# Local attention: queries in rows, the sum as a 65th column, and results transposed for the output

## What is computed

```python
def local_attention(q, k, v):           # per head; window of 128 queries, 256 keys
    sim = einsum('bhwid,bhwjd->bhwij', bq, bk)
    mask = (i < j) | (i > j + WINDOW) | (j == -1)
    sim = where(mask, -finfo.max, sim)
    attn = softmax(sim, axis=-1)
    out = einsum('bhwij,bhwjd->bhwid', attn, bv)
...
h = shift_token(x); q, k, v = split(h @ wqkv, 3)
q, k = l2norm(q) * qs, l2norm(k) * ksc; q, k = rotary_xpos(q, k)
x = x + local_attention(q, k, v) @ wo
x = x + feed_forward(x)                 # layer norm, w1, gelu gate, w2
```

## Time and profile before

| | |
|---|---|
| median of 3 runs (lowest to highest) | 1937.51 us (1932.22 to 1951.54) |
| the profiled execution, its time | 1935.36 us |
| its span from the first instruction to the last | 1933.9 us |
| TensorE clock granted, mean | 0.937 of 2.4 GHz |
| PE busy | 1773.7 us (92%) |
| PE weight loads busy | 1350.9 us (70%) |
| DVE, ACT, POOL busy | 1146.3 (59%), 982.9 (51%), 862.8 us (45%) |

### The profile page before, as it was taken

How to read it: one execution, slowest core, us unless ns; L and a number is a source line. 1 busy time by engine, 2 the same in 40 slices (tenths; PEclk the granted TensorE clock), 3 DMA queues, 4 the chain that set the end, 5 groups by cost and what they waited for, 6 DMA issues and landing times. The chain is left out here.

```text
span 1933.9 us, 42804 instructions
## 1 busy us (share of the span) xinstructions
PE 1773.7 (92%) x14072; PEld 1350.9 (70%) x14072; DVE 1146.3 (59%) x2863; ACT 982.9 (51%) x1898; POOL 862.8 (45%) x895
## 2 busy tenths in 40 slices
PE   6999999999569999999969999689999999879997
PEld 4566665666347777777758888467777777678886
DVE  5567766667367667666633333666666776325554
ACT  2655656655336555555543444345555655434443
POOL 3333334333246655555632333445556665325544
PEclk7888989998679999999988999889999999979999
DMA  5333344334010000000021222201000000212221
GB/s 149 108 109 121 105 131 123 115 111 132 22 35 12 33 33 33 33 33 22 0 89 55 65 65 88 66 12 33 33 33 1 32 33 22 78 54 77 87 87 44
DMA packets 103736, 121.29 MB, mean 63 GB/s; under 512 B 23386, under 2 KB 75780, under 8 KB 103684
## 3 DMA queue, kind: packets, MB, share of 16 engines
q1 hardware_dynamic: 96772, 95.45, 16.3%
q0 software_dynamic: 6912, 25.17, 3.7%
HBM read 82.55 MB, written 37.77 MB: 62 GB/s over the span
## 5 line engine op out<-in xcount | busy, mean ns | idle before, releaser
L417 ACT ACTIVATE a_PT<-a_c 128x384 f32<-128x384 f32 (+1 forms) x384 | 185.9, 524 | 135.1 <-PE a_c L644 104.8
L457 DVE TENSOR_REDUCE a_negm<-a_x 128x2 f32<-128x256 f32 (+3 forms) x256 | 199.9, 816 | 78.9 <-PE a_x L605 76.0
L882 POOL TENSOR_TENSOR work<-work 128x512 f32<-128x512 f32 x128 | 164.5, 1287 | 149.8 <-DVE work L1032 148.7
L1050 DVE CUSTOM_DVE_ANT_0 l_x<-l_x,window 128x256 f32<-128x256 f32 (+1 forms) x512 | 184.7, 424 | 31.8 <-PE l_x L1147 31.6
L1557 DVE SCALAR_TENSOR_TENSOR m_hid<-m_a,mw_b,m_gate 128x512 f32<-128x512 f32 x96 | 72.0, 750 | 197.8 <-ACT m_gate L1495 169.2
L1452 POOL TENSOR_TENSOR m_hid_lo<-m_hid,m_hid_hi 128x512 fp32r<-128x512 f32 x80 | 102.8, 1294 | 185.2 <-ACT m_hid_hi L1506 185.0
L1081 PE MATMUL l_f<-w_hi,tails 128*128 128x512 f32 x384 | 168.0, 437 | 13.8 <-DVE work L1032 10.7
L965 ACT ACTIVATE l_PT<-l_c 128x512 f32<-128x512 f32 (+1 forms) x256 | 125.3, 542 | 87.8 <-PE l_c L1187 84.3
L1082 PE MATMUL l_f<-w_hi,tails 128*128 128x512 f32 x384 | 154.4, 402 | 0.0
L1083 PE MATMUL l_f<-w_lo,tails 128*128 128x512 f32 x384 | 153.9, 401 | 0.0
L896 POOL TENSOR_TENSOR l_PS<-l_PT 128x768 f32<-128x768 f32 x64 | 119.8, 1872 | 58.7 <-ACT l_PT L965 58.7
(11 more groups left out here) (240 smaller groups left out, 5124.8 us busy)
## 6 DMA issues: line engine op xcount, KB each, us to landing
a_Q<-qk_parts SPq DMA_DIRECT2D x192, 64.0 KB, 2.1
a_K<-qk_parts SPq DMA_DIRECT2D x192, 64.0 KB, 2.1
qk_parts<-a_qk_hi SPq DMA_DIRECT2D x32, 256.0 KB, 2.2
qk_parts<-a_qk_lo SPq DMA_DIRECT2D x32, 256.0 KB, 2.1
after_attn<-rows_out POOLq DMA_DIRECT2D x16, 512.0 KB, 5.2
xin<-after_attn SPq DMA_DIRECT2D x32, 256.0 KB, 3.1
m_xr<-after_attn SPq DMA_DIRECT2D x16, 512.0 KB, 4.0
xin<-in_L_attn_x SPq DMA_DIRECT2D x8, 512.0 KB, 3.5
```

Of the source, the lines that this page charges most:

```text
L417: nc.scalar.activation(PT[:, p // PG % 2, 2 * (p % PG) + hh, QOFF[t]:QOFF[t] + nq], SC[hh][:, 0:nq], ACT.Exp, scale=AD ** -0.5).then_inc(e ...
L457: dve.tensor_reduce(negm[:, q, 2 * p:2 * p + 2], MX[i % 2][:, :, 0:nk], AX.X, ALU.max, negate=True).then_inc(max_done, 1)
L882: pool.tensor_tensor(t1[:, par, w, :], t1[:, par, w, :], t2[:, par, w, :], ALU.add)\
L1050: m = dve.tensor_tensor_reduce(out=o, in0=o, in1=mask, scale=-1.0, scalar=-NEG, op0=ALU.add, op1=ALU.min, accum_out=negm[:, q + t, p // 2, ...
```

## The change

Values are kept with a 65th column of ones behind each head's 64 features (`V[P, TB, FH, 65]`). In `pv` the exponentials become the loaded operand (128 keys by 128 queries) and the 65 columns of `V` stream: queries stand in the rows of the result, and column 64 is the sum. For each of 4 blocks of queries, 2 heads and 1 or 2 blocks of keys that is 14 matmuls in place of 8. Steps `ps`, `sv` and `z` are gone. DVE takes two reciprocals of 128x4 and multiplies twice 128x256 (`zn`). A new step `zr` transposes the four blocks of the pair's result on PE into `OB`; ACT writes `zh` and a full copy `zf` from there (`zs`), and POOL subtracts. The next `pv` waits for these copies (`zh_done`), since `OB` is written by both. `STEPS` is written in a new order.

```diff
-        V = sb("V", [P, TB, INNER])
-        ones = sb("ones", [P, FD])
+        FC = FD + 1
+        V = sb("V", [P, TB, FH, FC])
...
+        ZB = [t[:, 0:4 * FC].rearrange("p (t h c) -> p t h c", t=2, h=2) for t in (OB, SB)]
...
-                    elif name == "ps":
-                        pool.wait_ge(exp_done, 2 * (b * UNITS + 2 * i + 2))
-                        pool.wait_ge(o_full, b * PAIRS + max(i - 1, 0))
-                        pool.tensor_tensor(PS[:, i % 2], PT[:, i % 2, :, 1:TB, 0:P], PT[:, i % 2, :, 0:TB - 1, P:2 * P],
-                                           ALU.add).then_inc(ps_done, 1)
...
-                        pool.tensor_tensor(zl[:, i, :], zt[:, i, :], zh[:, i, :], ALU.subtract).then_inc(zl_done, 1)
+                        pool.tensor_tensor(zl[:, i, :], zf[:, i % 2, :], zh[:, i, :], ALU.subtract).then_inc(zl_done, 1)
...
-                        act.wait_ge(z_done, b * PAIRS + i + 1)
-                        nc.scalar.activation(zh[:, i, :], zt[:, i, :], ACT.Identity).then_inc(zh_done, 1)
-                    elif name == "z":
-
-                        act.wait_ge(o_full, b * PAIRS + i + 1)
-                        act.wait_ge(z_done, b * PAIRS + max(i - 1, 0))
-                        nc.scalar.activation(rr[:, i % 2, :], SB[:, :], ACT.Ln).then_inc(ln_done, 1)
-                        act.wait_ge(ln_done, b * PAIRS + i + 1)
-                        nc.scalar.activation(rr[:, i % 2, :], rr[:, i % 2, :], ACT.Exp, scale=-1.0).then_inc(rr_done, 1)
+                        act.wait_ge(zt_full, b * PAIRS + i + 1)
+                        act.wait_ge(zl_done, b * PAIRS + max(i - 1, 0))
+                        nc.scalar.activation(zh[:, i, :], OB[:, :], ACT.Identity)
+                        nc.scalar.activation(zf[:, i % 2, :], OB[:, :], ACT.Identity).then_inc(zh_done, 1)
...
-                        dve.tensor_tensor(zt[:, i, :], OB[:, :], rr[:, i % 2, :], ALU.mult).then_inc(z_done, 1)
+                        dve.wait_ge(o_full, b * PAIRS + i + 1)
+                        for n in range(2):
+                            dve.reciprocal(rc[:, n], ZB[n][:, :, :, FD]).then_inc(rc_done, 1)
+                        for n in range(2):
+                            dve.wait_ge(rc_done, 2 * (b * PAIRS + i) + n + 1)
+                            m = dve.tensor_tensor(zt[:, i, 2 * n:2 * n + 2], ZB[n][:, :, :, 0:FD],
+                                                  rc[:, n].unsqueeze(3).to_broadcast([P, 2, 2, FD]), ALU.mult)
+                        m.then_inc(z_done, 1)
...
-                        pe.wait_ge(z_done, b * PAIRS + i)
+
+                        pe.wait_ge(zh_done, b * PAIRS + i)
+                        pe.wait_ge(mrow_done, b * 2 + (1 if i == 0 else 2))
...
-                                pe.matmul(OB[rows, P * j:P * j + nq], V[:, j, FD * h:FD * h + FD],
-                                          PT[:, i % 2, hh, j, 0:nq], start=(j == 0), stop=(j == TB - 1),
-                                          skip_group_check=True)
-                    elif name == "sv":
...
-                            m = pe.matmul(SB[rows, P:S].rearrange("p (t q) -> p t q", q=P), ones[:, :],
-                                          PS[:, i % 2, hh, :, :], start=True, stop=True, skip_group_check=True)
+                                for j in range(max(t - 1, 0), t + 1):
+                                    m = pe.matmul(ZB[t // 2][:, t % 2, hh, :], PT[:, i % 2, hh, j, P * (t - j):P * (t - j) + P],
+                                                  V[:, j, 2 * i + hh, :], start=(t % 2 == 0 and hh == 0 and j == max(t - 1, 0)),
+                                                  stop=(j == t), skip_group_check=True)
                         m.then_inc(o_full, 1)
+                    elif name == "zr":
+                        pe.wait_ge(z_done, b * PAIRS + i + 1)
+                        for t in range(TB):
+                            m = pe.transpose(OB[:, P * t:P * t + P], zt[:, i, t].rearrange("p h d -> p (h d)"),
+                                             K["ident"][:, :])
+                        m.then_inc(zt_full, 1)
```

More of the change, by code:

```diff
@@ L813, in local_attention @@
         STEPS = [s.rsplit(":", 1) for s in """
[L814 to L818, removed]
+            sm:4 f_x:0 f_xe:0 st:0 sm:5 f_qk:0 f_qe:0 f_qk:1 f_qe:1 st:1 sm:6 f_qk:2 f_qk:3 pv:0 f_qk:4 f_iv:0
+            f_qe:2 f_qe:3 zn:0 f_iv:1 f_qe:4 sm:7 st:2 zr:0 f_qk:5 zs:0 f_qe:5 f_iv:2 f_qk:6 mt:1 f_qe:6 st:3 f_qk:7
+            xr:0 f_qe:7 st:4 pv:1 f_iv:3 zn:1 st:5 zr:1 zs:1 st:6 f_t:0 f_te:0 pv:2 f_t:1 zn:2 f_te:1 st:7 f_sm:0
+            f_t:2 zr:2 f_te:2 zs:2 f_sm:1 f_t:3 f_te:3 pv:3 f_sm:2 f_v:0 zn:3 f_sm:3 f_v:1 zr:3 zs:3 f_v:2 f_mt:0
+            f_v:3 out:0""".split()]
         STEPS = [(name, int(i)) for name, i in STEPS]
@@ L865, in _ @@
                 pool.memset(least[:, 1:2], 1e-24).then_inc(least_set, 1)
-                pool.memset(ones[:, :], 1.0).then_inc(small, 1)
+                pool.memset(V[:, :, :, FD:FC], 1.0).then_inc(ones_set, 1)
                 pool.memset(xt_hi[:, 1, 0:1].bitcast(F32), 0.0).then_inc(small, 1)
@@ L870, in _ @@
                 pool.wait_ge(pick_zero, 1)
-                pool.wait_ge(small, 3)
+                pool.wait_ge(small, 2)
                 for hh in range(2):
@@ L948, in do @@
                         act.wait_ge(front_full, b * NF + V_AT + i + 1)
-                        nc.scalar.activation(V[:, i, :], FB[i % 2][:, :], ACT.Identity).then_inc(v_done, 1)
+                        nc.scalar.activation(V[:, i, :, 0:FD], FB[i % 2][:, :].rearrange("p (h d) -> p h d", d=FD),
+                                             ACT.Identity).then_inc(v_done, 1)
                     elif name == "f_te":
@@ L1108, in do @@
                         pe.wait_ge(own.lo_done, KT)
-                        pe.wait_ge(small, 3)
+                        pe.wait_ge(small, 2)
                         if i == 0:
@@ L1153, in do @@
                         pe.wait_ge(max_done, 2 * (b * UNITS + 4 * i + 4))
[L1155 removed]
+                        pe.wait_ge(z_done, b * PAIRS + i)
                         if name == "f_mt" and not isinstance(b, int):
@@ L1196, in do @@
                         pe.wait_ge(exp_done, 2 * (b * UNITS + 2 * i + 2))
-                        pe.wait_ge(z_done, b * PAIRS + i)
+                        pe.wait_ge(zh_done, b * PAIRS + i)
+                        pe.wait_ge(mrow_done, b * 2 + (1 if i == 0 else 2))
                         pe.wait_ge(y_done, b * TB)
                         pe.wait_ge(v_done, b * TB + TB)
-                        for j in range(TB):
-                            nq = P if j == TB - 1 else 2 * P
+                        pe.wait_ge(ones_set, 1)
@@ L1202, in do @@
+                        for t in range(TB):
                             for hh in range(2):
-                                h, rows = 2 * i + hh, slice(FD * hh, FD * hh + FD)
-                                pe.matmul(OB[rows, P * j:P * j + nq], V[:, j, FD * h:FD * h + FD],
-                                          PT[:, i % 2, hh, j, 0:nq], start=(j == 0), stop=(j == TB - 1),
-                                          skip_group_check=True)
-                    elif name == "sv":
[L1209 to L1214, removed]
-                            pe.matmul(SB[rows, 0:P], ones[:, :], PT[:, i % 2, hh, 0, 0:P], start=True, stop=True,
-                                      skip_group_check=True)
-                        for hh in range(2):
-                            rows = slice(FD * hh, FD * hh + FD)
-                            m = pe.matmul(SB[rows, P:S].rearrange("p (t q) -> p t q", q=P), ones[:, :],
-                                          PS[:, i % 2, hh, :, :], start=True, stop=True, skip_group_check=True)
-                        m.then_inc(o_full, 1)
@@ new lines, in do @@
+                                for j in range(max(t - 1, 0), t + 1):
+                                    m = pe.matmul(ZB[t // 2][:, t % 2, hh, :], PT[:, i % 2, hh, j, P * (t - j):P * (t - j) + P],
+                                                  V[:, j, 2 * i + hh, :], start=(t % 2 == 0 and hh == 0 and j == max(t - 1, 0)),
+                                                  stop=(j == t), skip_group_check=True)
+                        m.then_inc(o_full, 1)
+                    elif name == "zr":
+                        pe.wait_ge(z_done, b * PAIRS + i + 1)
+                        for t in range(TB):
+                            m = pe.transpose(OB[:, P * t:P * t + P], zt[:, i, t].rearrange("p h d -> p (h d)"),
+                                             K["ident"][:, :])
+                        m.then_inc(zt_full, 1)
```

16 lines of the change are left out of this document (6 added, 10 removed).

## The result

| | before | after |
|---|---|---|
| median (lowest to highest), us | 1936.05 (1932.22 to 1951.54), 4 runs | 2015.22 (1995.48 to 2020.69), 4 runs |
| the profiled execution, us | 1935.36 | 2017.19 |
| its span, us | 1933.9 | 2015.7 |

The changed kernel takes 1.0396 times as long, with a 95% interval of 1.0338 to 1.0454. The forecast was 2000 us with a range of 1965 to 2045: the sign and the range hold, and the middle is 15 us low.

A forecast was written before the change was run, and what follows sets the result against it. PE alone was taken to bound the loop: 3.7 us more a batch over 16 batches gives +59 us, plus 5 us of waits on 1935.4 us, 2000 us in all; range 1965 to 2045 us.

The forecast's parts named there:

- The load's slot: New pv on PE: each 128 x 128 f32 load takes 0.110 us, 28 of them 3.08 us a pair.
- the first rival: New pv: streams set the pace, loads hidden or half as long; 39 us less, 1896 us; chance 0.04.
- The third: Rival on new pv: loads and streams don't overlap, 4.68 us a pair, 162 us more, 2097 us; chance 0.05.
- the fourth rival: PE's loop: the clock falls in pv, or a wait of some 3 us a batch opens; 2046 us; chance 0.12.
- `zr`: New step on PE: 4 transposes at 0.11 us each, 0.44 us a pair (0.42 to 0.51).
- Switches: Changes of array split on PE: 30 to 24 a batch at 0.18 us each, 1.1 us less.
- Net on PE: PE's time in the loop: 3.7 us more a batch, +59 us over 16 batches, before waits.
- The new waits: PE: zr waits for zn, next pv for zh and zf; 0.3 us a batch, +5 us (2 to 16).
- The new order: STEPS on PE: the order gives back 1.1 us a batch through 6 fewer changes of array split.
- The other engines: POOL, ACT and DVE: changes cost nothing because PE covers them, though DVE gains 2.6 us a batch.
- "PE alone sets the loop": First local attention's loop: PE, busy 347.68 of 350 us, sets the time; an edit counts by PE's time.
- "PE isn't full": PE's loop: loads busy only 266.93 of 350 us, so extra work disappears; time stays at 1935 us; chance 0.05.

The follow-up runs named there:

- e1: The changed kernel with each pv matmul streaming 126 columns of V in place of 65: 2012.8 us, 1.0442 times before.
- e2: The changed kernel's instructions, with steps put back in the order of before as far as possible: 2049.98 us, 1.0613 times before.
- e5: The kernel before, all its instructions, in an order made from the new one, sv and z right behind pv: 2101.69 us, 1.0865 times before.
- e3: The kernel before without ps, sv and z, so the result is not divided by the sums: 1922.47 us, 0.9924 times before.
- e6: The changed kernel with each pv matmul split into two that load 64 queries each: 1924.75 us, 0.9928 times before.
- e9: The changed kernel with each pv matmul split into four that load 32 queries each: 1981.97 us, 1.0197 times before.

## Why the prediction was right

**The load's slot** was the term that carried the sum, and it was right: 3.08 us forecast from 9.38/44/2 and the twelve of the earlier trace rows, and 3.08 measured with no switch at its end, 3.14 in the mean of the four pairs. That the load and not the stream is what counts was shown by e1, and the first rival (1896 us) falls with it. The third, loads and streams one after the other, falls too: 4.68 us was its price. Of the fourth rival neither half came: the clock is 1.00 in the loop, and the waits are those below.

**`zr`** was forecast at 0.44 us without switches; `zr:1` takes 743.52 - 742.49 - 0.37 = 0.66 us with them and without the wait behind it, and `zr:3`, which has no switch on either side, 0.35. So the transposes were priced 0.09 us a pair too high.

**Switches**: 1.1 us a batch less was forecast. Before, `pv` and `sv` took 6.56 + 4.02 = 10.58 us a batch, 1.30 more than the 4 x 2.32 without switches; after, `pv` and `zr` take 15.05, 0.97 more than 4 x 3.52, of which 0.37 is the wait behind `zr:1` and 0.11 one behind `zr:2`. So 1.30 - 0.49 = 0.8 us less there; the other steps have 0.2 less, most of it waits. That is about 0.9 by the prices of the prediction, but only some 0.5 if a `zr` without switches is taken at the measured 0.35. The counts, 30 and 24, are right by the trace; the price of one switch was not tested alone, and what the switches gave back is the least certain term of the sum.

**Net on PE**: 3.7 us a batch forecast plus 0.3 of waits, 4.27 measured in the first layer and 4.55 in the second. The switches gave back some 0.6 less than forecast, the transposes cost some 0.4 less, and each `pv` 0.06 more. 16 times 4.27 is 68 us where I had 64; the second layer's period adds the rest of the 70.6.

**The new waits** were sized right, 0.6 us a batch against 0.36 before, but stand elsewhere: neither `zr` for `zn` nor `pv` for `zh`, but `st:6` for exponentials that are queued on ACT.

**The new order** I priced by its switches alone. e2 shows it to be worth 2.5 us a batch with a difference of only 2 switches: its value is mostly waits avoided. It did no harm to the sum, since each kernel stands in an order made for its work; e5 shows what it costs where that isn't so.

**The other engines** were put at nothing, and rightly, up to the 0.37 us at `st:6`. DVE's part was sized too high: `zn` takes 0.98 us a pair where 1.2 to 1.35 was forecast, so that DVE gains 1.2 us a batch and not 2.6.

**"PE alone sets the loop"** is the step that was wrong in its generality. It held for the question asked, work added (after, e1). e3 shows that in the old order DVE's maxima and ACT's exponentials were just as late as PE: of 4.0 us taken off only 0.7 came back. A table with one wait of 2.3 us doesn't say how far the next bound is.

**"PE isn't full"**, the rival from the loads' busy share, fell: 76% before, 85% after (297.31 of 350), and the period grew by the full price. e6, with 82%, is 5 us a batch faster. The Trainium skill, Perfetto Trace Analysis, section Identifying the Most-Contended Engine, judges TensorE's headroom by this share and by the arithmetic done against the peak. For the share this trace doesn't agree: neither level told what time was to be had.

**The 15 us** by which the middle was low: about 6 are the loop (70.6 against 64 with the two layers as measured), the rest lies within what the unchanged first attention varies.

**Where the loss comes from**, then: not from the layout, but from loading 128 columns at a time. With halves the same layout and order are 0.7% faster than before (0.3 to 1.2%), the best version here in full precision. That is less than the 1% that I called measurable, but the two layers of the profiles agree: 950.2 us against 962.5. `pv` and `zr` then take 7.13 + 2.50 = 9.63 us a batch, 0.95 less than the 10.58 of `pv` and `sv`.

## What to carry to other kernels

Where the streamed side is short, price a matmul by its load, from a row with almost nothing streamed, and try to cut a 128-column load into two halves of the array before giving up a layout. A profile in which one engine is always busy prices added work; before counting on work removed, find how late the next engine's results come, for they may be just in time. And look at the instruction queue's packets, and at the branch that ends a pass, when an edit multiplies instructions inside a loop.

## What the hardware showed that I had not expected

- Half loads of 128 x 64 in f32 with 65 columns streamed run two at a time: 0.064 us for two, against 0.110 for one whole load (e6).
- Quarters bring next to nothing more: 1.73 against 1.79 us a pair, 0.0155 us in the mean for each of 112 matmuls, which start in fours 56 ns apart (e9). It isn't a limit on instruction starts, since the four start within 21 ns.
- Instructions were fetched again in every pass of e9's loop: 2.44 MB of instructions in place of 0.56, with 3.3 to 3.8 us for PE's branch back in place of 0.2 and stalls of up to 3.9 us on PE.
- Streams of 65 and of 126 columns cost the same behind a whole load (3.08 and 3.13 us a pair, e1).
- The first attention, with the same instructions, took from 523.5 to 550.0 us; the granted clock was 0.89 near the first and 0.84 at the second.
